# A transformer block on one core: stages of pieces by one rule, two subtractions on another engine

## What is computed

```
x = x + layernorm(attention(layernorm(x), w_q, w_k, w_v, w_o))
x = x + layernorm(ffn(layernorm(x), W_r, W_k, W_v, mu_r, mu_k))

attention: q, k, v = x @ w.T; softmax(q k.T * 0.25) v per head; concat @ w_o.T
ffn:       x_prev = x shifted by one token, zero first
           xr = mu_r * x + (1 - mu_r) * x_prev;  xk likewise with mu_k
           sigmoid(xr @ W_r.T) * (relu(xk @ W_k.T) ** 2 @ W_v.T)
```

## Time and profile before

| | us |
|---|---|
| median of three runs | 1254.45 |
| lowest, highest | 1248.7, 1254.75 |
| the profiled execution: its time | 1254.75 |
| its span (first to last instruction) | 1252.7 |
| PE busy | 1203.4 (96%) |
| ACT busy | 1058.8 (85%) |
| DVE busy | 806.1 (64%) |
| POOL busy | 193.4 (15%) |

### The profile page before, as it was taken

How to read it: one execution, slowest core, us unless ns; L and a number is a source line. 1 busy time by engine, 2 the same in 40 slices (tenths; PEclk the granted TensorE clock), 3 DMA queues, 4 the chain that set the end, 5 groups by cost and what they waited for, 6 DMA issues and landing times.

```text
span 1252.7 us, 25690 instructions
## 1 busy us (share of the span) xinstructions
PE 1203.4 (96%) x10604; PEld 650.2 (52%) x10604; DVE 806.1 (64%) x1841; ACT 1058.8 (85%) x1405; POOL 193.4 (15%) x292
## 2 busy tenths in 40 slices
PE   8989999999999999999999999999999999999997
PEld 5534555455545555455554555445545555535454
DVE  7652756857576775758658575775767567464657
ACT  4669898899989987898888989889988998999882
POOL 2000112021210202112110211202021020112121
PEclk9989999999999998999999999999999999999999
DMA  4455473416532185123833066431771129400000
GB/s 156 123 143 152 100 139 68 119 33 144 110 72 85 52 172 100 40 80 96 154 74 95 26 135 121 93 93 52 140 123 44 52 70 172 98 2 18 18 19 17
DMA packets 61797, 112.70 MB, mean 90 GB/s; under 512 B 6512, under 2 KB 31344, under 8 KB 61616
## 3 DMA queue, kind: packets, MB, share of 16 engines
q1 hardware_dynamic: 61360, 109.60, 38.5%
q10 hardware_dynamic: 288, 1.05, 0.3%
HBM read 68.42 MB, written 41.94 MB: 88 GB/s over the span
## 4 chain that ended last, share of the span: by engine, by line
PE 75%; DVE 18%; ACT 2%; issue 2%; DMA 1%; POOL 1%; SPq 0%; DVEq 0%
PE O L526 30%; PE M L508 22%; PE M L465 21%; DVE sth L818 2%; PE M L435 2%; ACT PT L616 1%; DVE B L1034 1%; PE M L407 1%; DVE A L826 1%; DVE B L781 1%; DVE A L992 1%; DVE scratch L1072 1%; DVE scratch L992 1%; DVE p L781 1%; DVE A L954 1%
## 5 line engine op out<-in xcount | busy, mean ns | idle before, releaser
L616 ACT ACTIVATE PT<-M 128x1024 f32<-128x1024 f32 x1274 | 1001.9, 864 | 149.3 <-PE M L508 139.1
L508 PE MATMUL M<-QS,KS 50*128 50x512 f32 x2048 | 500.8, 421 | 20.6 <-DVE On L843 13.4
L526 PE MATMUL O<-PT,V 128*17 128x512 f32 x4096 | 496.0, 601 | 0.4 <-ACT PT L616 0.4
L508 PEld LDWEIGHTS M<-QS,KS 50*128 50x128 f32 x2048 | 223.3, 185 | 278.4 <-ACT PT L616 238.5
L526 PEld LDWEIGHTS O<-PT,V 128*17 128x17 f32 x4096 | 93.7, 97 | 233.4 <-issue 217.3
L465 PE MATMUL M<-xnT,WH 64*128 64x512 f32 x496 | 144.8, 408 | 1.0 <-DVE p L781 0.8
L1098 DVE SCALAR_TENSOR_TENSOR A<-Z,M 128x512 f32<-128x512 f32 x30 | 20.6, 688 | 124.1 <-PE M L465 124.1
L1218 POOL TENSOR_TENSOR scratch<-scratch 128x512 f32<-128x512 f32 x30 | 37.4, 1247 | 397.4 <-DVE scratch L1072 397.4
L465 PE MATMUL M<-WH,B 64*128 64x256 f32 x480 | 85.0, 287 | 8.9 <-DVE B L781 8.9
L1196 POOL TENSOR_SCALAR veh<-mvh 128x2 f32<-128x2 f32 x96 | 21.4, 223 | 450.9 <-DVE mvh L821 449.1
L465 PE MATMUL M<-WH,xnT 64*128 64x256 f32 x480 | 84.8, 285 | 2.4 <-issue 2.4
(11 more groups left out here) (154 smaller groups left out, 1602.5 us busy)
## 6 DMA issues: line engine op xcount, KB each, us to landing
scr<-p SPq DMA_DIRECT2D x124, 256.0 KB
QS<-scr SPq DMA_DIRECT2D x56, 256.0 KB, 6.1
KS<-scr SPq DMA_DIRECT2D x56, 256.0 KB, 10.2
QS<-scr SPq DMA_DIRECT2D x70, 128.0 KB, 5.9
KS<-scr SPq DMA_DIRECT2D x68, 128.0 KB, 7.5
xA<-x_dram SPq DMA_DIRECT2D x16, 512.0 KB, 7.0
xB<-x_dram SPq DMA_DIRECT2D x16, 512.0 KB, 7.6
out_dram<-xB SPq DMA_DIRECT2D x15, 512.0 KB, 3.2
```

The lines of the kernel that those rows point to most:

```text
L508: e.matmul(PM[bank[i, j]], KS[qd][rows, pair, kt * 128:kt * 128 + 128], QS[qd][rows, pair, hf * 512:hf * 512 + 512], start=True, stop=True) \
L526: ins = e.matmul(PO[32 * j:32 * j + 17, :], V[b % 2][:, kt, 4 * qd + j, :], PT[i % 3][:, j, :], start=(kt == 0), stop=(kt == 7))
L616: e.activation(PT[i % 3][:, j:k + 1, :], PB[:, at:at + len(numbers), :], ACT.Exp, scale=SCALE) \
```

## The change

The two tables of steps are replaced by a rule. A piece with further stages enters a list; at each step at most two of those that were waiting get one stage each, and return to the list if they have more. `stages_of` says how many there are. `LN1_AT` goes from (3, 5, 26, 28) to (2, 6, 13, 16). And two subtractions, the low part of `cT` (stage 2 of a quad) and the low part of `C` for xk (stages 1 and 2 of z1), are issued on POOL where DVE issued them; the two units at the end keep theirs on DVE where it has a path of its own. The assignment of pieces to steps and banks stays, and with it the order on PE, ACT and SP.

```diff
--- before.py
+++ after.py
@@ -46,7 +46,9 @@
 TAIL = ("y0", "y1", "z0", "z1", "k0", "k1", "r0", "r1", "v0", "v1")
 
 SENT = ("Q00", "K00", "K01", "Q10", "K10", "K11", "Q01", "Q11")
-LN1_AT = (3, 5, 26, 28)
+
+STAGES = {"y": 3, "v": 2, "T": 2}
+LN1_AT = (2, 6, 13, 16)
 SPREAD_AT = (12, 18, 26)
 FIRST_SPREADS = {2: [(1, (0, 1), (0,))], 6: [(1, (1,), (1,))], 7: [(2, (0, 1), (0,))], 8: [(2, (1,), (1,))],
                  10: [(3, (0, 1), (0,)), (3, (1,), (1,))], 16: [(qd, (0,), (1,)) for qd in range(4)]}
@@ -59,19 +61,17 @@
     return u // 2 if word == "V3" else u - 1
 
 
-def later_at(piece, i):
-
+def stages_of(piece):
     word, n = piece
-    if word[0] == "y":
-        return (i + 1, i + 2) if n >= UNITS - 2 else (i, i + 2) if word == "y0" else (i + 2, i + 3)
-    if word == "z1" and n < UNITS - 2:
-        return i + 1, i + 1, i + 6, i + 8
-    return dict(k1=(i + 2,), v0=(i + 1,), v1=(i + 1,), T00=(i + 1,), T10=(i + 1,)).get(word, ())
-
-
-def quad_at(g):
-
-    return ((8 * g + 9 if g > 0 else 8,), (8 * g + (11 if g > 1 else 9),) * 2, (8 * g + 9,), (8 * g + 9,) * 2)[g % 4]
+    if word == "quad":
+        return 3 if n % 2 else 2
+    if word in ("T01", "T11"):
+        return 1
+    if word == "z1":
+        return 5 if n < UNITS - 2 else 1
+    if word == "k1":
+        return 2
+    return STAGES.get(word[0], 1)
 
 
 def plan():
@@ -100,11 +100,9 @@
         for row, steps in ((0, at), (1, then)):
             for part, j in enumerate(steps):
                 halves[j][row] = ((word, batch), 2 if len(steps) < 2 else part)
-    ends, rests = [], [[] for _ in range(STEPS + 32)]
-    for g in range(STEPS // 8 - 1):
-        for stage, j in enumerate(quad_at(g)):
-            rests[j].append((("quad", g), stage + 1))
+    ends, rests, waiting = [], [], []
     for i in range(STEPS):
+        rested, waiting = waiting, []
         end = []
         if halves[i][1] and halves[i][1][1]:
             end.append((halves[i][1][0], 0))
@@ -112,10 +110,16 @@
             end += [((word, 0), 0) for word in ALONE_IN[i]]
         if turns[i]:
             end.append((turns[i], 0))
+        done = i if i < PAIRED else i - 1
+        rest = [(("quad", done // 8), 0)] if done % 8 == 7 else []
+        waiting += [(piece, 1) for piece, _ in end + rest if stages_of(piece) > 1]
+        for piece, stage in rested[:2]:
+            rest.append((piece, stage))
+            if stage + 1 < stages_of(piece):
+                waiting.append((piece, stage + 1))
+        waiting[:0] = rested[2:]
         ends.append(end)
-        for stage, j in enumerate(later_at(end[0][0], i) if end else ()):
-            rests[j].append((end[0][0], stage + 1))
-    assert not any(rests[STEPS:])
+        rests.append(rest)
     return halves, turns, ends, rests
 
 
@@ -906,8 +910,6 @@
                     if u:
                         p.wait_ge(("piece", ("y1", u - 1)))
                     e.tensor_copy(cT[0][:, cols], at[:, :]).then_inc(*note(("cT_hi", g)))
-                    lower(cT[1][:, cols], at[:, :], cT[0][:, cols].bitcast(F32), ("cT_hi", g), ("T_read", g),
-                          ("cT", u, m, 0), ("cT", u, m, 1))
 
             def last_quad():
                 g = STEPS // 8 - 1
@@ -1025,7 +1027,6 @@
                     if u:
                         p.wait_ge(("piece", ("v1", u - 1)))
                     e.tensor_copy(C[0][:, both], A[:, both]).then_inc(*note(("xk_hi", u, c)))
-                    lower(C[1][:, both], A[:, both], C[0][:, both].bitcast(F32), ("xk_hi", u, c), ("xk", u, c))
                 else:
                     c, both = stage - 3, slice((stage - 3) * 512, (stage - 2) * 512)
                     diff = scratch[(1 + 4 * u + c) % 3][:, :]
@@ -1164,7 +1165,8 @@
                     elif piece[0][0] != "V":
                         after_QK(piece, stage, True)
                 for piece, stage in RESTS[i]:
-                    after[piece[0][0]](piece, stage)
+                    if i < STEPS - 1 or piece[0] != "quad":
+                        after[piece[0][0]](piece, stage)
                 if u == 0 and 7 <= s < 11:
                     parted(("wr", "wo", "wkf", "wvf")[s - 7])
                 if u == 0 and s in (4, 5, 6, 7):
@@ -1209,8 +1211,21 @@
 
             def after(piece, stage):
                 word, n = piece
-                if word[0] == "y" and stage < 2:
+                if word == "quad":
+                    if stage == 2:
+                        u, m = n // 4, n % 4 // 2
+                        cols = slice(512 * m, 512 * m + 512)
+                        p.wait_ge(("cT_hi", n))
+                        e.tensor_tensor(cT[1][:, cols], T[n % 2][:, :], cT[0][:, cols].bitcast(F32), ALU.subtract) \
+                            .then_inc(*up(pool_wrote, ("T_read", n), ("cT", u, m, 0), ("cT", u, m, 1)))
+                elif word[0] == "y" and stage < 2:
                     rsqrt(("y", "xn2")[stage], n, int(word[1]))
+                elif word[0] == "z" and 0 < stage < 3:
+                    c = stage - 1
+                    cols = slice(512 * c, 512 * c + 512)
+                    p.wait_ge(("xk_hi", n, c))
+                    e.tensor_tensor(C[1][:, cols], A[:, cols], C[0][:, cols].bitcast(F32), ALU.subtract) \
+                        .then_inc(*up(pool_wrote, ("xk", n, c)))
                 elif word[0] == "k" and stage == 0:
                     t = int(word[1])
                     r = scratch[(1 + 4 * n + 2 + t) % 3][:, :]
```

## The result

| | before | changed |
|---|---|---|
| median us | 1254.6 (4 runs) | 1300.03 (4 runs) |
| lowest to highest | 1248.7 to 1254.95 | 1298.01 to 1300.86 |
| profiled execution, its span | 1252.7 | 1299.2 |

The ratio is 1.0371, with a 95% interval of 1.0338 to 1.0405: slower. The forecast was 1293, within 1264 to 1307.

A forecast was written before the change was run, and what follows sets the result against it. PE, 96% busy, was taken to stall where DVE empties PSUM banks late. Terms summed to +40.9 us, less 2.9 for the lock let go early, about +38: 1252.7 + 38 + 2.05 gave 1293 us, range 1264 to 1307.

The forecast's parts named there:

- s=2 and s=4, even: Steps 2 and 4 of even 32-step units: earlier copy of T00 gains 15.5 us, later emptying of T01 costs 5.4.
- s=12, odd and even: Step 12: y1's stages moved ahead of Q's emptying and T10's copy; +10.5 us in odd units, +4.2 in even.
- s=20 and s=22, even: Step 20, even units: Q01 emptied late behind DVE's other stages and port waits; stall 3.85 us each, +23.1 in six units.
- s=20 and s=22, odd: Step 20, odd units: V1 emptied late; stall 3.4 us in six units, 2.5 in unit 13, +22.9 in all.
- s=4, odd: Step 4, odd units: LN1's statistics ahead of Q10 delay its emptying; with the lock 1.8 us late, five units, +7.5.
- The bank windows: Two rotating PSUM banks: DVE has 2.3 us from a piece's completion to empty it, 0.9 of them for other work.
- The lock: DVE and POOL exclude each other on a shared port, so casts beside POOL's subtractions wait; without it +12.4 us, not +40.9.
- The case without a lock: Rival: POOL's subtractions do not hold up DVE, sum +12.4, 1267 us; chance 0.17.
- The clock: Rival: PE's clock halves in the new s=20 stalls, 1.5 us in eight of them, +12, 1305 us; chance 0.16.
- LN1 at s=16: Odd units: LN1's four normalizations, ahead of V0, wait 0.8 to 1.0 us more behind POOL's first C subtraction.
- Absorption: Half of each new stall, without a lock, is absorbed, giving 1244 us; chance 0.06 together with the 1222 us case.
- the faster rival: Emptying is not late at s=20, s=12 and s=4; only gains remain, -32.7, 1222 us; chance 0.06 including some absorption.

The follow-up runs named there:

- `rule_q_first`: Changed kernel with the stages of s=18 moved behind the emptying of Q01 or V1 and the fourth z stage behind the next emptying; 1247.0 us, ratio 0.994.
- `narrow`: Changed kernel with POOL's two subtractions cut to 8 of 512 columns, the rest of the low parts set to zero once; 1267.6 us, ratio 1.010.
- `rule_ln_old`: Changed kernel with `LN1_AT` back to (3, 5, 26, 28); 1293.7 us in one run.

## Why the prediction was right, term by term

Measured terms are differences of the same periods in the two profiles, times their number.

| term | predicted us | measured us |
|---|---|---|
| s=2 and s=4, even | -10.1 | -10.9 |
| s=12, odd and even | +14.7 | +13.7 |
| s=18, even | -2.5 | -2.8 |
| s=24 | -12.9 | -12.2 |
| s=20 and s=22, even | +23.1 | +33.2 |
| s=20 and s=22, odd | +22.9 | +23.6 |
| s=4, odd | +7.5 | +6.2 |
| first unit | -1.8 | -1.4 |
| unit 7, a pause of PE's issue at s=18 | 0 | -2.7 |
| lock let go early | -2.9 | (in the rows above) |
| sum | +38 | +46.7 (span +46.5) |

**The bank windows.** Right. Every place named is the place that moved, and `rule_q_first` shows the largest of them by itself: s=20 from 9.91 to 4.38.

**The lock.** Right in mechanism, and near in size at s=20. There the sum had 8.1 us for it in even units and 15.2 in odd ones, 23.3 in all. Where the clock stayed full, `narrow` has s=20 at 6.60 and 5.17, stalls of 2.2 and 0.8, for the changed kernel's 3.7 (by the emptying) and 2.5: 9 and 12 us. The other 11 of `narrow`'s 32 are seven falls of the clock less. At s=4 the sum had 5.2 us for what POOL's subtraction does; `narrow` left s=4 as it was, since the cast there waits for POOL's addition, so that share was put down to the wrong operation. The case without a lock, 1267 us, is within a microsecond of what `narrow` took, in part by chance: `narrow` still has three falls of the clock at s=20 and the slow cast ahead of s=4, and the sum had neither. At s=20 of even units the emptying was late by 8.43 - 4.74 = 3.7 for 3.85.

**The clock** is the term that was mis-sized. The forecast had it at nothing and left it to a rival with 12 us. In unit 4 the stall by emptying is 3.7, and the period is 5.25 longer: 1.6 us are the clock's. The odd units show this price by itself. In five of them PE's longest gap at s=20 is 2.2 us, and the period takes 6.85 and 6.88 where the clock stayed full (units 3 and 11), and 8.40 to 8.49 where it fell (units 1, 5 and 9). Over the six even units the clock took 33.2 - 6 x 3.7 = 11 us, and in the odd ones 23.6 less seven stalls of 2.5, near 6. The changed kernel has 11 halved stretches before its end for 4, all at the stalls of s=20 but the first. The outcome, 1300, lies between forecast and rival, nearer to the rival.

One reading of the earlier trace rows was off by this. The prediction has slow periods of 6.98, 5.42 and 5.48 behind the dear forms of s=2. By the first score product, s=2 of unit 6 took 8.34 and the period behind it 5.28, and in units 2 and 12 s=2 took 7.66 and 7.73 with an undisturbed 4.39 behind. The sums of the pairs are the same, so the term of -15.5 stands. Three terms differ a little from their own figures, by about 1 us together: 2.7 where s=18 has 2.5, 7.7 where s=4 of odd units has 7.5, and for s=4 of even units without the lock 0.34 each (5.3 against 4.96) where the text has 0.45.

**LN1 at s=16** was the other error, the other way. Its four normalizations did take 2.35 us beside POOL's subtraction, for 1.4:

```profile
464.25 2.35 DVE L779 TENSOR_SCALAR xA<-xA,mv,rs 128x256 f32<-128x256 f32 x4
466.52 0.68 DVE L884 COPY V<-M 128x512 f32<-128x512 f32 x1
```

but the V0 behind them was complete only 2.44 after 463.85. They filled a wait that I had counted already, and delayed V0 by 0.2, not 0.95. `rule_ln_old` agrees: 0.2 in the unit with the full clock. So the 1293 was near in part by luck: the clock's 17 us were missing, 0.95 in six units were too much, and a pause in the profile of the kernel before took off another 2.7; together that is nearly all of the 8.7 between the two sums.

**Absorption**, the faster rival's way out, did not happen at the places that can be read without the clock. At s=4 of unit 5 Q10 is empty 1.86 into the period for a deadline of 0.32, and the period is 1.54 longer than 4.38.

## What to carry to other kernels

When an engine's order decides how early a shared buffer is given back, write down for each such buffer when it is complete and when it is wanted again, and count only the work between them; busy shares say nothing about it, and a rule that spreads work evenly puts it into just these windows. What can wait belongs where the engine waits anyway: 12 us came from two numbers of a table. Moving work to a second engine paid off (10 us) once the order was right, although the two engines held each other up.

## What the hardware showed that I had not expected

- The granted clock fell to the half level in stalls as short as 1.8 us, in three of six that were otherwise alike (the earlier trace rows have one with and one without), and in ten of the thirteen stalls of s=20 in the changed kernel. Stalls that look the same can differ by this alone: 1.6 us between units 3 and 5 of one execution.
- Holding each other up is dear on both sides. In the changed kernel's profile POOL's subtraction for cT took 1.28 us ahead of s=4, and 1.70 at s=18 and s=20, behind a DVE operation with two inputs; a DVE cast took 0.43 alone and up to 1.39 beside it. It still was hardly dearer than the 0.69 us subtraction on DVE at s=20, where Q01 is empty at 8.43 against 8.35, and cheaper at s=4.
- tensor_scalar takes part: 256 columns with two scalars from pointers took 0.41 us alone, and one of the four at s=16 took 1.38.
